# Reading layer 0's accumulators two pairs later, in a four-layer graph network on one core

## The chip, the core and the metric

One core of a Trainium2 chip runs the whole program in one launch. The metric is the device time of that launch in microseconds, taken over several executions; one execution is also recorded by the hardware profiler, and all rows below come from it. The engines are TensorE (PE, with its weight loads shown as PEld), VectorE (DVE), ScalarE (ACT), GpSimd (POOL) and SyncE (SP), which here only issues transfers.

## What is computed

`x` is 4096 x 128 and `adj` 4096 x 4096, both fp32. Four graph layers follow each other, each with a residual and a layer norm:

```python
x = _layernorm(x + _L0_gnn_ref(x, adj, L0_gnn_W), axis=-1)
x = _layernorm(x + _L1_gnn_ref(x, adj, L1_gnn_W, L1_gnn_b), axis=-1)
x = _layernorm(x + _L2_gnn_ref(L2_gnn_t, x, adj, L2_gnn_alpha, L2_gnn_beta), axis=-1)
x = _layernorm(x + _L3_gnn_ref(x, adj, L3_gnn_W_msg, ...), axis=-1)
```

Layer 0, which the change concerns, is a hyperbolic one. Its core is two products with the same matrix and then work on single rows:

```python
XW = mobius_matvec(W, X)
gamma = 2.0 / jnp.maximum(1.0 - jnp.sum(XW * XW, axis=-1, keepdims=True), EPS)
nominator = A_hat @ (gamma * XW)
denominator = _clamp_abs(A_hat @ (gamma - 1.0))
m = mobius_scalar_mul(0.5, nominator / denominator)
r = A_hat.sum(-1, keepdims=True)
return expmap0(jax.nn.relu(logmap0(mobius_scalar_mul(r, m))))
```

Layer 1 multiplies the same matrix, with degrees to the power -1/2 on both sides, by the new `x`.

## The kernel before

The adjacency matrix is cut into 8 slabs of 512 rows. TensorE needs it turned, so layer 0 turns each 128 x 128 block once, uses it, and stores it to `adj_t` in HBM; layers 1 and 3 load `adj_t` back.

**Layer 0's loop** is the same on all engines: `n` counts the pairs of column blocks, 16 pairs to a slab (`m = n % 16`), 128 in all. For each pair:
- SyncE loads tiles of 1 MB (L314), one for two pairs, a slab ahead, and stores the turned ones (L358) from three slots.
- TensorE turns eight blocks into one of two strips in PSUM (`turn0`, L473), four pairs ahead of the multiply (`AHEAD = 4`).
- ScalarE copies the strip into a slot of `full` (`full0`, L732), then writes its high part, rounded to fp32r, into `part_h` (`high0`, L739).
- VectorE writes the rest into `part_l` (`low0`, L1199).
- TensorE multiplies (`multiply0`, L490, L491 and L493), with `Y` (260 columns: 128 of data and two more, in high and low part) as the moving operand. The sums stand in four banks, the two of `acc` and the two of `mid`.

What ties the engines together: `turn0(n)` waits for `full0(n - 2)`, since there are two strips; `high0(n)` waits for `multiply0(n - 4)`, since `part_h` has eight slots; `multiply0(n)` waits for `low0(n)`; and the first multiply of a slab waits until the slab before has been read out.

**Reading the banks.** `read_acc0(s)` waits for the last multiply of slab `s`. ScalarE then copies two banks into `nat` (L745, L746) and VectorE the two others (L1206, L1207).

**The row chain.** From `nat` the slab's 512 rows go through some 40 small steps on ScalarE, VectorE and GpSimd (`rows0(k, s)`), each behind the one before by a semaphore that counts in the order of the list `ROWS`. The steps are hung into the next slab's loop by hooks: pair `m` runs `k = 2m` and `k = 2m + 1`. ScalarE has the square (L763), the logarithm (L767, with a table load), the relu (L771), a second square (L776) and the tanh (L780, with another table load). GpSimd has the sums (L974), the powers (L979, L981, L986, L989) and two products; VectorE everything else, from the degree steps (L1248 to L1253) to the layer norm. In the last slab GpSimd also scales `Y`'s groups for layer 1 (`y_scale`, L954) and writes their low parts (`y_low`, L961), and ScalarE writes their high parts (`y_high`, L723).

**Layer 1's loop** has 128 turns. ScalarE makes `high(1, n)` (L787), VectorE `low(1, n)` (L1320), TensorE multiplies (L512, L513, L521). The last slab's row chain is hung into its first 26 turns; ScalarE writes the last group of `Y` in turn 26.

Of the kernel before, what the change touches and what calls it, by code (L numbers as in the profile page):

```python
# [94 lines left out]
def build(nc, x, adj, w0, w1, b1, alpha, beta, w_msg, b_msg, w_ih, w_hh, b_ih, b_hh, out, scratch, dis_out):  # L95
    with ExitStack() as ctx:
# [584 lines left out]
        def _(act):  # L681
# [75 lines left out]
            def rows0(k, s):  # L757
                par = s % 2
                t, v, sc = t_of[par], v_of[par], sc_of[par]
                if k == 5:  # L760
                    act.wait_ge(row[par], row_before(0, s, "square"))
                    for q in range(Q):
                        last = act.activation(v[:, q, :], t[:, q, :], ACT.Square, accum_out=sc[:, SS, q:q + 1])  # L763
                    last.then_inc(row[par], 1)
                if k == 11:
                    act.wait_ge(row[par], row_before(0, s, "log"))
                    act.activation(sc[:, LOG, :], sc[:, RATIO, :], ACT.Ln).then_inc(row[par], 1)  # L767
                if k == 16:
                    act.wait_ge(row[par], row_before(0, s, "times_relu"))
                    for q in range(Q):  # L770
                        last = act.activation(t[:, q, :], t[:, q, :], ACT.Relu, scale=sc[:, SCL, q:q + 1])  # L771
                    last.then_inc(row[par], 1)
                if k == 17:
                    act.wait_ge(row[par], row_before(0, s, "square_u"))
                    for q in range(Q):
                        last = act.activation(v[:, q, :], t[:, q, :], ACT.Square, accum_out=sc[:, SS, q:q + 1])  # L776
                    last.then_inc(row[par], 1)
                if k == 19:
                    act.wait_ge(row[par], row_before(0, s, "tanh_u"))
                    act.activation(sc[:, H, :], sc[:, NRM, :], ACT.Tanh).then_inc(row[par], 1)  # L780
# [85 lines left out]
            for n in range(PAIRS * SLABS):  # L866
                s, m = n // PAIRS, n % PAIRS
                full0(n)
                high0(n)
                if s == 0 and 1 <= m <= GROUPS:  # L870
                    y_high(0, m - 1)
                if m == 1 and s > 0:
                    read_acc0(s - 1)
                if s > 0:
                    rows0(2 * m, s - 1)
                    rows0(2 * m + 1, s - 1)
                if s == SLABS - 1 and m >= 5 and m % 2 == 1:
                    y_high(1, (m - 5) // 2)
            read_acc0(SLABS - 1)
            for n in range(TURNS_ALL):  # L880
                high(1, n)
                if n == 4:
                    y_high(1, SLABS - 2)
                if 2 <= n < 26:
                    rows0(n + 1, SLABS - 1)
                if n == 26:
                    y_high(1, SLABS - 1)
                for k, s in hooks(1, n - ACT_LEAD):
                    rows1(k, s)
# [40 lines left out]
        def _(pool):  # L930
# [33 lines left out]
            def rows0(k, s):  # L964
                par = s % 2
                t, sc = t_of[par], sc_of[par]
                mine = slice(Q * s, Q * (s + 1))

                def before(name):
                    pool.wait_ge(row[par], row_before(0, s, name))  # L970
                if k == 3:
                    before("sum_parts")
                    pool.wait_ge(acc_read, acc_reads_done(0, s))
                    pool.tensor_tensor(t[:], nat[:, :, 0:D], nat[:, :, LO:LO + D], ALU.add).then_inc(row[par], 1)  # L974
                    before("sum_den")
                    pool.tensor_tensor(sc[:, DEN, :], nat[:, :, D], nat[:, :, LO + D], ALU.add).then_inc(row[par], 1)
                if k == 6:
                    before("norm")
                    pool.tensor_tensor(sc[:, NRM, :], sc[:, SS, :], half[:, 0:Q], ALU.pow).then_inc(row[par], 1)  # L979
                    before("deg_pow")  # L980
                    pool.tensor_tensor(sc[:, DEG, :], sc[:, SAFE, :], inv_half[:, 0:Q], ALU.pow).then_inc(row[par], 1)  # L981
                if k == 11:
                    before("dcol")
                    pool.tensor_tensor(dcol[:, mine], sc[:, DEG, :], sc[:, KEEP, :], ALU.mult).then_inc(row[par], 1)
                    before("dis")
                    pool.tensor_tensor(dis[:, mine], sc[:, ZERO, :], inv_half[:, 0:Q], ALU.pow).then_inc(row[par], 1)  # L986
                if k == 18:
                    before("norm_u")
                    pool.tensor_tensor(sc[:, NRM, :], sc[:, SS, :], half[:, 0:Q], ALU.pow).then_inc(row[par], 1)  # L989
                if k == 20:  # L990
                    before("times_u")
                    pool.tensor_tensor(t[:], t[:], wide(sc[:, SCL, :]), ALU.mult).then_inc(row[par], 1)
                    before("add_x")
                    pool.tensor_tensor(t[:], t[:], x_nat[:, mine, :], ALU.add).then_inc(row[par], 1)
                if k == 24:
                    layer_norm(0, s)
# [74 lines left out]
            for n in range(TURNS_ALL + HOOKS[1]):  # L1071
                if n < 24:
                    rows0(n + 3, SLABS - 1)
                if n == 4:
# [33 lines left out]
        def _(dve):  # L1108
# [127 lines left out]
            def rows0(k, s):  # L1236
# [8 lines left out]
                total = nat[:, :, D + 1]  # L1245
                if k == 5:
                    before("degrees")
# [5 lines left out]
                    dve.tensor_scalar(val(SIGN), val(DEN), 0.0, 2.0, ALU.is_ge, ALU.mult).then_inc(row[par], 1)  # L1253
                if k == 6:
                    before("abs_floor")
# [6 lines left out]
                                             ALU.mult).then_inc(row[par], 1)  # L1262
                if k == 8:
                    before("norm_den")
# [3 lines left out]
                    dve.tensor_scalar(val(UNIT_), val(NRM), MIN_NORM, None, ALU.max).then_inc(row[par], 1)  # L1268
                if k == 9:
                    before("artanh_a")  # L1270
# [7 lines left out]
                    dve.tensor_tensor(val(UNIT_), val(INV), val(INV_NRM), ALU.mult).then_inc(row[par], 1)  # L1278
                if k == 10:
                    before("ratio")  # L1280
# [4 lines left out]
                    dve.scalar_tensor_tensor(val(H), val(H), 1.0 / 3, val(Z), ALU.add, ALU.mult).then_inc(row[par], 1)  # L1285
                if k == 12:
                    before("series")
                    dve.scalar_tensor_tensor(val(SER), val(H), 1.0, val(CLIP), ALU.add, ALU.mult).then_inc(row[par], 1)
                if k == 13:
                    before("differ")  # L1290
# [3 lines left out]
                                             ALU.mult).then_inc(row[par], 1)  # L1294
                if k == 14:
                    before("artanh")
                    dve.scalar_tensor_tensor(val(ART), val(LOG), 0.5, val(SER), ALU.mult, ALU.add).then_inc(row[par], 1)
                    before("scale")
                    dve.scalar_tensor_tensor(val(SCL), val(ART), 0.5, total, ALU.mult, ALU.mult).then_inc(row[par], 1)
                if k == 15:  # L1300
                    before("scale_clip")
                    dve.tensor_scalar(val(SCL), val(SCL), ARTANH_MAX, -ARTANH_MAX, ALU.min, ALU.max).then_inc(row[par], 1)
                    before("scale_row")
                    dve.tensor_tensor(val(SCL), val(SCL), val(UNIT_), ALU.mult).then_inc(row[par], 1)
                if k == 18:
                    before("clamp_u")
                    dve.tensor_scalar(val(SS), val(SS), MIN_NORM ** 2, None, ALU.max).then_inc(row[par], 1)
                if k == 20:
                    before("inv_u")
                    dve.reciprocal(val(INV), val(NRM)).then_inc(row[par], 1)  # L1310
                    before("scale_u")
                    dve.tensor_tensor(val(SCL), val(H), val(INV), ALU.mult).then_inc(row[par], 1)
                if k in (22, 25):
                    layer_norm(0, (22, 25).index(k), s, lambda q: x_nat[:, Q * s + q, :])

# [138 lines left out]
            for n in range(PAIRS * SLABS):  # L1454
                s, m = n // PAIRS, n % PAIRS
                if s == 0 and m < GROUPS:
                    y_scale(m)
                low0(n)
                if m == 1 and s > 0:
                    read_acc0(s - 1)  # L1460
                if s > 0:
                    rows0(2 * m, s - 1)
                    rows0(2 * m + 1, s - 1)
            read_acc0(SLABS - 1)
            for n in range(TURNS_ALL):
                low(1, n)
                if n < 24:
                    rows0(n + 3, SLABS - 1)
                for k, s in hooks(1, n - DVE_LEAD):
                    rows1(k, s)  # L1470
# [59 lines left out]
```

## Time and profile before

| | |
|---|---|
| time, median of 3 runs | 1453.44 us (1452.11 to 1456.87) |
| profiled execution | 1456.6 us |
| its span in the trace | 1454.8 us |
| TensorE matmul busy | 1320.9 us (91%) |
| VectorE, ScalarE busy | 1072.7 us, 1073.5 us (74% each) |
| GpSimd busy | 570.1 us (39%) |
| mean granted TensorE clock | 0.969 of full |
| DMA, mean over the span | 284 GB/s |

The span is the time from the first to the last recorded instruction; the execution's own time holds some 1.8 us more. Layer 0's slabs lie between about 32 and 445 us. Matmuls are pipelined, so a busy TensorE is not one at its peak.

### The profile page before, as it was taken

Reading aid. Unit: us, or ns where it says so; the run is one execution under the profiler, and the core shown is the slowest. Engines: PE = TensorE matmul, PEld = TensorE weight load, DVE = VectorE, ACT = ScalarE, POOL = GpSimd, SP = SyncE. Lnnn points to the kernel's source line nnn. Section 1 sums busy time; section 2 is a strip of 40 time slices with the busy share of each in tenths; the row PEclk is TensorE's granted clock in tenths of the full one; section 3 lists DMA queues with packets and bytes.
Section 4 is the critical chain, followed back from the end, with each engine's and each line's share of the span. In section 5 each row is a group of like instructions: output and inputs, shape, how many; then the busy total and the mean of one; then the engine's idle time right before and its main releaser. Section 6 shows DMA issues by size and latency. Waiting matters only on the chain.

```text
span 1454.8 us, 21041 instructions
## 1 busy us (share of the span) xinstructions
PE 1320.9 (91%) x7640; PEld 1023.7 (70%) x7640; DVE 1072.7 (74%) x1936; ACT 1073.5 (74%) x1376; POOL 570.1 (39%) x441
## 2 busy tenths in 40 slices
PE   6998988998888989997799999999999889999995
PEld 5988988988887667774366666666666657767663
DVE  6844545555567889996687888978888869787874
ACT  6876877787687667774888888788887647767764
POOL 3312212221353544335177677676776650000010
PEclk9999999999999999999899999999999989999998
DMA  9998989989876878893578787787877848877850
GB/s 306 402 339 303 349 321 322 348 327 325 307 276 222 303 284 302 324 353 148 217 278 301 268 306 266 280 293 284 299 269 238 276 173 364 343 268 268 284 200 22
DMA packets 114808, 413.08 MB, mean 284 GB/s; under 512 B 10000, under 2 KB 23568, under 8 KB 90128
## 3 DMA queue, kind: packets, MB, share of 16 engines
q1 hardware_dynamic: 106256, 407.54, 77.3%
q10 hardware_dynamic: 8448, 4.20, 1.0%
q8 instruction: 60, 0.98, 0.3%
q14 instruction: 44, 0.36, 0.1%
HBM read 340.40 MB, written 71.30 MB: 283 GB/s over the span
## 4 chain that ended last, share of the span: by engine, by line
PE 53%; DVE 18%; ACT 17%; issue 6%; POOL 5%; DMA 1%; POOLq 0%; ACTq 0%; DVEq 0%; SPq 0%
DVE part_l L1320 7%; PE strip_b L576 5%; PE acc L493 5%; PE mid L493 5%; PE acc L521 4%; PE acc L512 4%; PE acc L513 4%; PE strip_b L473 3%; PE strip_a L473 3%; ACT part_h L787 3%; PE acc L593 3%; ACT arena L814 3%; PE acc L590 2%; PE acc L591 2%; ACT arena L732 2%
## 5 line engine op out<-in xcount | busy, mean ns | idle before, releaser
L1320 DVE TENSOR_TENSOR part_l<-arena,part_h 128x1024 fp32r<-128x1024 f32 x256 | 326.3, 1310 | 58.2 <-ACT part_h L787 56.9
L1033 POOL TENSOR_TENSOR part_l<-arena,part_h 128x512 fp32r<-128x512 f32 x237 | 303.8, 1294 | 156.1 <-ACT part_h L825 156.1
L787 ACT ACTIVATE part_h<-arena 128x1024 fp32r<-128x1024 f32 x256 | 264.7, 1055 | 120.9 <-PE acc L521 111.1
L1199 DVE TENSOR_TENSOR part_l<-arena,part_h 128x1024 fp32r<-128x1024 f32 x128 | 161.0, 1267 | 132.9 <-ACT part_h L739 132.1
L825 ACT ACTIVATE part_h<-arena 128x512 fp32r<-128x512 f32 x256 | 157.7, 623 | 94.4 <-DVE arena L1394 93.7
L512 PE MATMUL acc<-part_h,Y 128*128 128x512 f32 x512 | 220.6, 431 | 3.7 <-ACT part_h L787 3.3
L513 PE MATMUL acc<-part_h,Y 128*128 128x512 f32 x512 | 204.5, 399 | 0.0
L1001 POOL TENSOR_TENSOR sc<-sc,power 128x4 f32<-128x4 f32 x32 | 49.3, 1542 | 329.8 <-DVE sc L1225 329.8
L576 PEld LDWEIGHTS strip_b<-ident,arena 128*128 128x128 f32 x1024 | 127.0, 142 | 69.0 <-DVE arena L1394 19.5
L521 PE MATMUL acc<-part_l,Y 128*128 128x512 f32 x512 | 164.8, 403 | 11.1 <-DVE part_l L1320 10.8
L576 PE MATMUL strip_b<-ident,arena 128*128 128x128 f32 x1024 | 157.4, 277 | 15.7 <-DVE arena L1394 10.6
L739 ACT ACTIVATE part_h<-arena 128x1024 fp32r<-128x1024 f32 x128 | 135.6, 1060 | 31.3 <-PE mid L493 28.5
L493 PE MATMUL acc<-Y,part_h 128*128 128x260 f32 x496 | 145.3, 344 | 0.0
L493 PE MATMUL mid<-Y,part_h 128*128 128x260 f32 x496 | 144.1, 341 | 0.0
L814 ACT ACTIVATE arena<-arena,neg_peak 128x2048 f32<-128x2048 f32 x64 | 127.4, 1991 | 3.5 <-DVE neg_peak L1371 3.5
L820 ACT ACTIVATE arena<-arena,weight 128x2048 f32<-128x2048 f32 x64 | 127.1, 1991 | 2.4 <-DVE weight L1384 2.4
L491 PE MATMUL acc<-Y,part_l 128*128 128x130 f32 x512 | 127.5, 249 | 0.0
L521 PEld LDWEIGHTS acc<-part_l,Y 128*128 128x128 f32 x512 | 94.8, 190 | 40.5 <-DVE part_l L1320 20.1
L590 PE MATMUL acc<-part_h,Y 128*128 128x512 f32 x256 | 122.9, 480 | 0.0
L512 PEld LDWEIGHTS acc<-part_h,Y 128*128 128x128 f32 x512 | 98.0, 191 | 34.2 <-issue 7.2
L513 PEld LDWEIGHTS acc<-part_h,Y 128*128 128x128 f32 x512 | 98.0, 191 | 28.6 <-issue 8.4
L491 PE MATMUL mid<-Y,part_l 128*128 128x130 f32 x512 | 116.6, 228 | 0.0
(257 smaller groups left out, 2776.3 us busy)
## 6 DMA issues: line engine op xcount, KB each, us to landing
arena<-adj_t SPq DMA_DIRECT2D x128, 1024.0 KB, 4.9
arena<-in_adj SPq DMA_DIRECT2D x64, 1024.0 KB, 7.9
adj_t<-arena SPq DMA_DIRECT2D x64, 1024.0 KB, 6.3
arena<-in_adj SPq DMA_DIRECT2D x128, 512.0 KB, 5.9
part_h<-adj_t SPq DMA_DIRECT2D x64, 512.0 KB, 5.2
part_l<-adj_t SPq DMA_DIRECT2D x64, 512.0 KB, 5.6
scratch<-v ACTq DMA_DIRECT2D x8, 256.0 KB, 10.4
arena<-scratch SPq DMA_DIRECT2D x8, 256.0 KB, 5.3
```

The costliest lines, as they stand in the source:

```text
L491: last = pe.matmul(acc0[q][:, 0:LO], part_l[:, slot, mine], Y[:, j, 0:LO], start=False, stop=False)
L493: last = pe.matmul(acc0[q][:, 0:YW], part_h[:, slot, mine], Y[:, j, :], start=False, stop=stop)
L512: pe.matmul(to, Y[:, j, 0:D], h, start=j == 0, stop=False)
L513: pe.matmul(to, Y[:, j, LO:LO + D], h, start=False, stop=False)
L521: last = pe.matmul(to, Y[:, j, 0:D], part_l[:, 2 * (n % 4) + j % 2, :], start=False, stop=j == NB - 1)
L576: last = pe.transpose(strip_b[:, b % 2, P * q:P * (q + 1)], unit_in[:, place, P * (j % 8):P * (j % 8 + 1)], ident[:])
L787: act.activation(flat(part_h[:, slot:slot + 2, :]), turned_pair(n), ACT.Copy).then_inc(high_done, 1)
L814: act.activation(mine, mine, ACT.Exp, bias=neg_peak[:, r % 2:r % 2 + 1], accum_out=exp_sum[:, r % 2, h:h + 1]).then_inc(exps, 1)
L825: act.activation(part_h[:, b % 4, :], mixed[b % G_SLOTS], ACT.Copy).then_inc(high_done, 1)
L1033: pool.tensor_tensor(part_l[:, b % 4, :], mixed[b % G_SLOTS], part_h[:, b % 4, :].bitcast(F32), ALU.subtract).then_inc(low_done, 1)
L1199: dve.tensor_tensor(flat(part_l[:, slot:slot + 2, :]), full_pair(n), flat(part_h[:, slot:slot + 2, :]).bitcast(F32), ALU.subtract).then_in ...
L1320: dve.tensor_tensor(flat(part_l[:, slot:slot + 2, :]), turned_pair(n), flat(part_h[:, slot:slot + 2, :]).bitcast(F32), ALU.subtract).then_ ...
```

## The change

Three things move; no instruction is added or taken out.

1. The read of a slab's banks moves from pair 1 of the next slab, behind that pair's high and low part, to pair 3, on ScalarE between the copy and the high part, on VectorE ahead of the low part.
2. The hooks of the row chain move: the first GpSimd step from 3 to 7, the degree steps and the square from 5 to 8, the steps at 6 to 9, and every later one by two, which is one pair.
3. The last slab's read, so far ahead of all of layer 1, moves to turn 3 of layer 1, ahead of that turn's high and low part, and its hooks start one or three turns later.

```diff
@@ ScalarE, rows0 (square, log, relu, square_u, tanh_u)
-                if k == 5:
+                if k == 8:
...
-                if k == 11:
+                if k == 13:
...
-                if k == 16:
+                if k == 18:
...
-                if k == 17:
+                if k == 19:
...
-                if k == 19:
+                if k == 21:
@@ ScalarE, the loops
                 full0(n)
+                if m == 3 and s > 0:
+                    read_acc0(s - 1)
                 high0(n)
                 if s == 0 and 1 <= m <= GROUPS:
                     y_high(0, m - 1)
-                if m == 1 and s > 0:
-                    read_acc0(s - 1)
...
-            read_acc0(SLABS - 1)
             for n in range(TURNS_ALL):
+                if n == 3:
+                    read_acc0(SLABS - 1)
                 high(1, n)
...
-                if 2 <= n < 26:
-                    rows0(n + 1, SLABS - 1)
+                if 5 <= n < 26:
+                    rows0(n + 2, SLABS - 1)
@@ GpSimd, rows0 (sums; norm, deg_pow; dcol, dis; norm_u; times_u, add_x; layer norm)
-                if k == 3:
+                if k == 7:
...
-                if k == 6:
+                if k == 9:
...
-                if k == 11:
+                if k == 13:
...
-                if k == 18:
+                if k == 20:
...
-                if k == 20:
+                if k == 22:
...
-                if k == 24:
+                if k == 26:
@@ GpSimd, layer 1's loop
-                if n < 24:
-                    rows0(n + 3, SLABS - 1)
+                if 3 <= n < 24:
+                    rows0(n + 4, SLABS - 1)
@@ VectorE, rows0: 5 -> 8, 6 -> 9, 8 -> 10, 9 -> 11, 10 -> 12, 12 -> 14, 13 -> 15, 14 -> 16,
@@ 15 -> 17, 18 -> 20, 20 -> 22, (22, 25) -> (24, 27)
@@ VectorE, the loops
+                if m == 3 and s > 0:
+                    read_acc0(s - 1)
                 low0(n)
-                if m == 1 and s > 0:
-                    read_acc0(s - 1)
...
-            read_acc0(SLABS - 1)
             for n in range(TURNS_ALL):
+                if n == 3:
+                    read_acc0(SLABS - 1)
                 low(1, n)
-                if n < 24:
-                    rows0(n + 3, SLABS - 1)
+                if 3 <= n < 24:
+                    rows0(n + 4, SLABS - 1)
```

## Rows read from the trace of the kernel before

**Rows 1.** The page: busy time of each engine, share of the span, instructions

```profile
PE 1320.9 (91%) x7640; PEld 1023.7 (70%) x7640; DVE 1072.7 (74%) x1936; ACT 1073.5 (74%) x1376; POOL 570.1 (39%) x441
```

**Rows 2.** Timeline of ScalarE, first reads of slabs: start, length, instruction, [idle before <-releaser]

```profile
82.51 0.39 ACT L745 ACTIVATE arena<-acc 128x260 f32<-128x260 f32 x1 [4.33 <-PE mid L493]
...
135.06 0.39 ACT L745 ACTIVATE arena<-acc 128x260 f32<-128x260 f32 x1 [4.33 <-PE mid L493]
...
186.10 0.39 ACT L745 ACTIVATE arena<-acc 128x260 f32<-128x260 f32 x1 [4.33 <-PE mid L493]
...
390.26 0.39 ACT L745 ACTIVATE arena<-acc 128x260 f32<-128x260 f32 x1 [4.33 <-PE mid L493]
...
444.92 0.39 ACT L745 ACTIVATE arena<-acc 128x260 f32<-128x260 f32 x1 [5.78 <-PE mid L493]
```

**Rows 3.** Timeline of TensorE over one undisturbed pair: multiply, transposes, next multiply

```profile
127.47 0.31 PE L491 MATMUL acc<-Y,part_l 128*128 128x130 f32 x1
...
129.41 1.04 PE L473 MATMUL strip_a<-ident,arena 128*128 128x128 f32 x8
...
130.20 0.31 PE L491 MATMUL acc<-Y,part_l 128*128 128x130 f32 x1
```

**Rows 4.** Timeline of all engines at a slab's boundary

```profile
134.69 0.33 PE L493 MATMUL mid<-Y,part_h 128*128 128x260 f32 x1
...
135.41 0.42 DVE L1207 COPY arena<-mid 128x260 f32<-128x260 f32 x1
135.61 1.03 ACT L732 ACTIVATE arena<-strip_a 128x1024 f32<-128x1024 f32 x1
```

**Rows 5.** Timeline of TensorE: transposes that came behind a gap, in layer 0

```profile
111.48 1.94 PE L473 MATMUL strip_a<-ident,arena 128*128 128x128 f32 x8 [1.81 <-ACT arena L732]
136.79 1.06 PE L473 MATMUL strip_a<-ident,arena 128*128 128x128 f32 x8 [1.76 <-ACT arena L732]
141.63 1.62 PE L473 MATMUL strip_b<-ident,arena 128*128 128x128 f32 x8 [1.92 <-ACT arena L732]
164.02 1.06 PE L473 MATMUL strip_a<-ident,arena 128*128 128x128 f32 x8 [1.46 <-ACT arena L732]
...
398.10 1.97 PE L473 MATMUL strip_b<-ident,arena 128*128 128x128 f32 x8 [3.19 <-ACT arena L732]
```

**Rows 6.** Timeline of ScalarE in a middle slab: row steps and a high part

```profile
139.39 0.31 ACT L763 ACTIVATE v<-t 128x128 f32<-128x128 f32 x1 [1.66 <-DVE sc L1253]
...
155.70 1.28 ACT L771 ACTIVATE t<-t,sc 128x128 f32<-128x128 f32 x4
...
159.24 1.06 ACT L739 ACTIVATE part_h<-arena 128x1024 fp32r<-128x1024 f32 x1
...
162.75 0.21 ACT L780 ACTIVATE sc<-sc 128x4 f32<-128x4 f32 x1 [1.16 <-POOL sc L989]
```

**Rows 7.** Windows: busy us of each engine, granted TensorE clock, DMA share, GB/s

```profile
142.00:145.40 3.40, 3.40 (x19) 3.40 (x17) 2.42 (x6) 3.37 (x4) 0.84 (x1) 0.51 0.87 320
```

**Rows 8.** Windows, same columns (PE, PEld, DVE, ACT, POOL): a later slab and slab 0

```profile
136.80:186.10 49.30, 45.88 (x384) 45.31 (x384) 25.87 (x63) 37.30 (x56) 9.94 (x10) 0.97 0.92 329
32.00:82.50 50.50, 48.19 (x400) 46.95 (x400) 37.91 (x44) 40.34 (x44) 12.28 (x8) 0.97 1.03 396
```

**Rows 9.** Timeline of VectorE: from the powers to the ratio step

```profile
146.82 0.16 DVE L1265 TENSOR_TENSOR sc<-sc 128x4 f32<-128x4 f32 x1 [0.90 <-POOL sc L981]
...
147.94 1.22 DVE L1199 TENSOR_TENSOR part_l<-arena,part_h 128x1024 fp32r<-128x1024 f32 x1
...
149.33 0.16 DVE L1285 SCALAR_TENSOR_TENSOR sc<-sc 128x4 f32<-128x4 f32 x1
```

**Rows 10.** Timeline at layer 1's first multiply and at its copy of Y

```profile
446.58 0.50 PE L512 MATMUL acc<-part_h,Y 128*128 128x512 f32 x1 [1.70 <-ACT part_h L787]
...
491.69 0.63 ACT L723 ACTIVATE Y<-arena 128x512 fp32r<-128x512 f32 x1 [2.73 <-POOL arena L954]
```

## What I predict, before any run of the change

> **What bounds the kernel now.** I read the page first, then a table by stage, then layer 0 instruction by instruction. The page gives TensorE 91% of the span and VectorE and ScalarE 74% each [rows 1]: a busy kernel in which only stretches that one engine holds up can be won back. The change touches layer 0's slabs and the first turns of layer 1, so the question is what ends the waits there.
>
> ScalarE's reads of the accumulators mark the slabs [rows 2]. They stand 52.55 us apart for the first slab (82.51 to 135.06), 51.04 for the next (135.06 to 186.10), and the four after it repeat it (390.26 - 186.10 = 4 x 51.04). The last takes 54.66 (390.26 to 444.92). Undisturbed, TensorE needs 2.73 us for a pair: 1.94 from its first multiply to the next pair's transposes, and 0.79 from there to the next multiply (127.47, 129.41, 130.20) [rows 3]. Sixteen pairs make 43.7 us. So 51.04 - 43.7 = 7.3 us of each slab is not TensorE's own work at full clock.
>
> Where it goes is in the gaps. At the boundary TensorE's last matmul starts at 134.69, ScalarE and VectorE read the banks at 135.06 to 135.83, ScalarE's copy of the slab's third pair comes only then (135.61), and the transposes that need its strip start at 136.79, after 1.76 us idle [rows 2, 4, 5]. The next gap is 1.92 us before 141.63: ScalarE stood at a row step (square, L763) for VectorE until 139.39, and made the next copy 1.2 us later [rows 5, 6]. The third is 1.46 us before 164.02, behind the tanh step, which waited for GpSimd until 162.75 [rows 5, 6]. Together 5.1 us. The rest is mostly clock: after the 1.92 us gap the granted clock is 0.51, the lower level of 1.2 GHz, for 3.4 us [rows 7]. Half of that, 1.7 us, is work not done. What is left, 0.5 us, goes at the three restarts.
>
> Is something else just behind TensorE? Slab 0 shows what DMA carries: 396 GB/s over 50 us at full TensorE pace, where a later slab has 329 [rows 8]. A slab moves 16.8 MB (eight loads and eight stores of 1 MB), so DMA alone needs 16.8 / 396 = 42.4 us.
>
> **The change, part by part.** Times below count from the start of the accumulator read, T; "copy", "high" and "low" of pair i are L732, L739 and L1199, i counted from the slab's first pair.
>
> *The read moves from after high 1 to between copy 3 and high 3.* No instruction is added or removed: two reads on each of two engines, 0.55 us of ScalarE and 0.77 of VectorE. TensorE runs transposes four pairs ahead. Now transposes 4 need copy 2, which is queued behind the read. After the change copy 2 and copy 3 are done before the last multiply ends, so transposes 4 follow it without a gap, and the read lies beside them. Multiply 0 starts when the read is done, 0.88, where the transposes alone would allow 0.59. Today it starts at 2.52 (transposes at 136.79, plus 0.79). So the boundary costs 0.3 instead of 1.93. Were the cover of these transposes gone, the read would cost its whole 0.8. High 3 is behind the read on ScalarE, low 3 behind it on VectorE (1.65 to 2.87), but multiply 3 needs low 3 only at 9.1, so nobody waits.
>
> *The row steps go two hooks on, most of them one pair.* I walked them with today's durations. TensorE, unhindered, starts transposes i+5 at 2.84 + 2.73i, and copy i+3 must be out by then. High 4 waits for multiply 0 and runs 3.10 to 4.16; VectorE's low 4 ends at 5.43, and behind it come the degree steps until 5.79. ScalarE does the square at 5.82, copy 5 from 7.00 to 8.00. Transposes 7 are due at 8.30: the 1.92 us gap is gone, with 0.2 to spare. The wait itself (1.66 us on ScalarE) stays, only its place is covered.
> - Logarithm, now at pair 6. GpSimd's two powers end at 10.0 (today VectorE takes up behind them at 146.82), low 5 at 10.36, and VectorE's chain takes 1.12 us before the next low (146.82 to 147.94), so until 11.39; low 6 and the ratio step end 1.55 us later (147.94 to 149.33 plus 0.16) [rows 9], at 12.94; the logarithm goes at 12.98, copy 7 ends at 14.09, due 13.76: TensorE loses 0.48 with the restart. Today this step costs nothing in a middle slab, because TensorE is at half clock just then and ScalarE catches up.
> - Relu and second square, now at pair 9. Highs 7, 8 and 9 are end to end at 2.00 us a pair, the relu starts at 19.16, copy 10 ends 3.5 us later, as today (155.70, and the high behind it at 159.24 [rows 6]), at 22.67, due 22.43: 0.39 lost.
> - Tanh, now at pair 10: high 10 starts at 22.70, the tanh 3.51 us later as today (159.24 to 162.75 [rows 6]), and copy 11 ends at 27.33, due 25.55: 1.93 lost with the restart, against 1.46 today.
> - From there ScalarE at 2.00 us a pair regains its lead on 2.73 before the slab ends, as now. The layer norm's steps stay three pairs from the multiply that would need VectorE.
>
> The slab becomes 43.7 + 0.3 + 0.48 + 0.39 + 1.93 = 46.8 us for 51.04: **4.26 us** won. Five middle slabs give 21.3; the first, to the same 46.8, gives 5.8.
>
> *Last slab.* GpSimd also scales Y for layer 1 there (L954). Three of the six scalings now fall before the read, and the 3.19 us gap before 398.10 [rows 5] goes the same way as the 1.92 one. But VectorE's chain for the logarithm meets another scaling as it does today, and ScalarE has three Y copies of some 0.5 us among the steps. My walk has gaps of 0.25, 2.1, 1.5 and 1.9 us, 5.8 in all, where today's slab is 54.66 - 43.7 = 11.0 over the pure pace: 5.2 won, the least certain term.
>
> *Clock.* That sum of 32.3 us has today's clock losses taken out and none put in. In today's layer 0, gaps of 1.81, 1.92 and more were followed by the lower clock, and of those of 1.76 and below only one, the first boundary's ([rows 5] has gaps of either kind: the eight transposes behind them take 1.06 us at full clock, more at the lower). My tanh gap of 1.93 is on the edge, and the walk is good to some 0.3 us, so I let four of seven slabs pay 1.7: 6.7 us back. Bounds: none, or seven times 1.7 = 11.8.
>
> *Layer 1's entry.* High 0 to 2 and low 0 to 2 now run before T. The first multiply starts at 0.9 for 1.66 [rows 10]: 0.75 won. Against that, the row chain of slab 7 is about 0.6 us later in time while TensorE is a turn further, and ScalarE's copy of the last group of Y already waits 2.73 us for GpSimd at turn 26 [rows 10]; the multiply behind it starts when that copy is out. The gain can be given back there. Bounds -0.8 to +1.0, taken as 0. SP's loads for layer 1 wait for low 1, now some 5 us earlier; layer 1's pace is VectorE's, so this is worth nothing.
>
> Sum: 32.3 - 6.7 + 0 = 25.6 us. The profiled execution took 1456.6 us (span 1454.8 and 1.8 around it), so 1431.0. It lay 3.2 above the median of the three runs; against 1453.4 the forecast is **1428**.
>
> **A page's rule against it.** The Trainium skill (DMA: Bandwidth & Descriptors, Specifications) gives a limit of about 358 GB/s of HBM traffic for one core. By it a slab could not be shorter than 16.8 / 358 = 46.9 us, what the walk gives; the transfers would be at their limit all the time, the stores late, and rival 2 the likeliest case. The trace does not agree: slab 0 runs at 396 GB/s [rows 8].
>
> **Rivals.**
> 1. *No clock loss* (chance 0.17). The tanh gap stays under the edge: 1453.4 - 32.3 - 0.5 = 1421. For it: today's 1.46 to 1.76 gaps inside a running stretch kept the clock. Against: the walk says 1.93. The Trainium skill (TensorE: Matmul & The Clock Gate, Why this matters for your kernels) counts as harmful only idle gaps longer than any in these middle slabs. By it this rival would be the forecast, 1421. The trace does not agree: the clock fell behind a gap of 1.92 us [rows 5, 7].
> 2. *DMA or ScalarE takes the place of the boundary* (0.12). The stores wait in three slots, copy i waits for them, and at 360 GB/s for today's 329 they land later. If DMA settles between the two rates, at 340 to 346 GB/s, a slab is 48.5 to 49.4 us, which leaves 1.6 to 2.5 of the 4.26, over seven slabs 11 to 18 with the surplus of the first and last less what their clock costs: 1437 to 1443. Against it: slab 0.
> 3. *It does not do what it says* (0.04). If slabs were held by transfers at today's rate, 16.8 MB at 329 GB/s is 51 us and the time stays, 1453. The gaps end on ScalarE's copy, not on a load; that speaks against it.
> 4. *Slower* (0.04). ScalarE's queue fills. It is busy 37.3 us a slab [rows 8] and waits 3.4 at row steps; from 43.7 on it sets the pace instead of TensorE, and with 51.04 the change loses. That takes 10 us more of waiting for VectorE and GpSimd per slab; if norm and logarithm both fall a pair later than walked (2 x 2.7) and the tanh two pairs, a slab is 52 us and the time 1460.
>
> The forecast itself has 0.63. **Numbers.** Its own range: 32.3 - 11.8 - 1 = 19.5 won to 32.3 - 3.3 + 0.8 = 29.8, so 1424 to 1434. With rival 1's low end (1420) inside, and a margin toward rival 2 for the 0.3 us per step of the walk (7 x 0.6 = 4), 1419 to 1438. A difference under 0.3% (4.4 us) can hardly be told from none here; faster 0.92, same 0.04, slower 0.04.
>
> **What would show it.** Right: reads 46 to 49 us apart in layer 0; no gap over 0.4 us before the transposes that follow the read; ScalarE's wait at L763's line still about 1.7 us but no TensorE gap after it; a gap near 2 us behind the tanh; a lower clock after it in some slabs; layer 1's first multiply 0.9 after T. Wrong: copies that wait for a store; a gap behind the logarithm over 1 us in middle slabs; a boundary gap in place of the old one because high 2 or copy 3 is late. The prediction would be wrong above all if the three gaps of the walk, each the difference of two long sums, grew by 1 us each.

## The result, and the profile after

The changed kernel takes 1429.97 us (1428.33 to 1432.67, four runs) where the kernel before takes 1453.55 in the same comparison: the ratio is 0.9836, with a 95% interval of 0.9814 to 0.9859. The forecast was 1428, with 1419 to 1438 around it. The profiled execution has a span of 1428.0 us for 1454.8, so 26.8 less; the forecast was 25.6.

The timeline of ScalarE in the changed kernel, first read of each slab, as in [rows 2] (the line number is the same, 745):

```profile
82.40 0.39 ACT L745 ACTIVATE arena<-acc 128x260 f32<-128x260 f32 x1 [0.69 <-PE mid L493]
...
129.13 0.39 ACT L745 ACTIVATE arena<-acc 128x260 f32<-128x260 f32 x1 [0.69 <-PE mid L493]
...
175.87 0.39 ACT L745 ACTIVATE arena<-acc 128x260 f32<-128x260 f32 x1 [0.69 <-PE mid L493]
...
224.21 0.39 ACT L745 ACTIVATE arena<-acc 128x260 f32<-128x260 f32 x1 [0.69 <-PE mid L493]
...
367.64 0.39 ACT L745 ACTIVATE arena<-acc 128x260 f32<-128x260 f32 x1 [0.69 <-PE mid L493]
...
418.60 0.39 ACT L745 ACTIVATE arena<-acc 128x260 f32<-128x260 f32 x1 [2.27 <-PE mid L493]
```

The distances are 46.73 and 46.74 for the first two slabs, 48.34 for the third, and with the reads at 270.95 and 319.30, which are not shown, 46.74, 48.35 and 48.34 for the next three; the last takes 50.96. Two things are to be seen. Layer 0 gives 26.2 of the 26.8 us (336.2 between first and last read for 362.4) in this trace. And there are two kinds of middle slab, 1.6 us apart. ScalarE's idle time at the read fell from 4.33 to 0.69: it comes there with its other work done.

The timeline of all engines at a boundary, for [rows 4]: the transposes start right behind the last multiply, the reads (to 129.48 + 0.42) lie beside them, and the first multiply starts 0.91 us behind T = 129.13. TensorE idles 0.28 us for it, before its weight load (PEld).

```profile
128.76 0.34 PE L493 MATMUL mid<-Y,part_h 128*128 128x260 f32 x1
128.93 1.03 PE L473 MATMUL strip_a<-ident,arena 128*128 128x128 f32 x8
129.48 0.42 DVE L1208 COPY arena<-mid 128x260 f32<-128x260 f32 x1
...
130.01 0.19 PEld L490 LDWEIGHTS acc<-Y,part_h 128*128 128x128 f32 x1 [0.28 <-issue]
130.04 0.36 PE L490 MATMUL acc<-Y,part_h 128*128 128x260 f32 x1
```

All transposes of TensorE that came behind a gap between the reads at 129.13 and 175.87, for [rows 5], and one of the next slab:

```profile
143.29 1.09 PE L473 MATMUL strip_b<-ident,arena 128*128 128x128 f32 x8 [0.24 <-ACT arena L732]
151.95 1.06 PE L473 MATMUL strip_a<-ident,arena 128*128 128x128 f32 x8 [0.26 <-ACT arena L732]
156.52 1.09 PE L473 MATMUL strip_b<-ident,arena 128*128 128x128 f32 x8 [1.64 <-ACT arena L732]
...
203.25 1.93 PE L473 MATMUL strip_b<-ident,arena 128*128 128x128 f32 x8 [1.63 <-ACT arena L732]
```

The gaps of 1.76 and 1.92 us are gone. Three are left, behind logarithm, second square and tanh. The last row explains the slabs of 48.3: behind a gap of the same length the transposes took 1.93 us for 1.09. The windows behind the two gaps (columns as in [rows 7]) show the clock, 1.00 of full in the one and 0.50, the level of 1.2 GHz, in the other:

```profile
157.00:159.70 2.70, 2.70 (x26) 2.70 (x25) 1.58 (x4) 2.67 (x4) 0.52 (x1) 1.00 0.96 361
...
203.80:206.50 2.70, 2.70 (x15) 2.70 (x14) 1.66 (x4) 2.67 (x4) 0.59 (x1) 0.50 1.05 400
```

ScalarE's timeline of the slab, for [rows 6], to hold against the walk:

```profile
134.96 0.31 ACT L763 ACTIVATE v<-t 128x128 f32<-128x128 f32 x1 [1.66 <-DVE sc L1254]
...
142.12 0.21 ACT L767 ACTIVATE sc<-sc 128x4 f32<-128x4 f32 x1 [0.58 <-DVE sc L1286]
...
148.30 1.28 ACT L771 ACTIVATE t<-t,sc 128x128 f32<-128x128 f32 x4
...
155.35 0.20 ACT L780 ACTIVATE sc<-sc 128x4 f32<-128x4 f32 x1 [1.16 <-POOL sc L990]
155.46 1.00 ACT L732 ACTIVATE arena<-strip_b 128x1024 f32<-128x1024 f32 x1
```

Less T these are 5.83, 12.99, 19.17, 26.22 and 26.33. The walk had 5.82, 12.98, 19.16, 26.21 and 26.33.

The last slab is a case of its own. Its window, in the same columns, beside that of a middle slab:

```profile
129.13:175.87 46.74, 44.52 (x386) 43.74 (x385) 26.88 (x64) 38.88 (x58) 11.50 (x10) 1.00 0.96 359
...
367.64:418.60 50.96, 44.35 (x352) 43.13 (x350) 32.69 (x65) 38.16 (x61) 28.29 (x20) 0.93 0.69 268
```

TensorE has 352 matmuls there for the 386 of a middle slab: the transposes run four pairs ahead, so the last four pairs of the layer have none beside them. And the clock is 0.93 of full, with two low stretches, 0.55 over 3.6 us behind a gap of 2.85 us (384.40) and 0.70 over 5.6 us behind one of 1.96 us (413.01). That is some 3.3 us of work not done.

### The profile page after: what moved, and what is told of

It is laid out like the page before. It is cut to its first block, busy times and chain, and to the rows that moved or that the text cites. A ratio compares the mean times of both kernels' runs of the same rounds, so it can differ in the third digit from the quotient of the medians.

```text
span 1428.0 us, 21041 instructions
## 1 busy us (share of the span) xinstructions
PE 1315.2 (92%) x7640; PEld 1017.7 (71%) x7640; DVE 1076.5 (75%) x1936; ACT 1072.9 (75%) x1376; POOL 577.5 (40%) x441
## 4 chain that ended last, share of the span: by engine, by line
PE 50%; DVE 19%; ACT 18%; issue 7%; POOL 4%; DMA 2%; POOLq 0%; ACTq 0%; DVEq 0%; SPq 0%
DVE part_l L1321 7%; PE strip_b L576 5%; PE acc L521 4%; PE acc L512 4%; PE acc L513 4%; PE acc L493 3%; PE mid L493 3%; ACT arena L732 3%; PE acc L593 3%; ACT arena L814 3%; DVE part_l L1200 3%; ACT part_h L787 2%; PE acc L590 2%; PE acc L591 2%; PE strip_b L473 2%
```

## The experiments

Each kernel was timed against the kernel before on the same chip. Nothing in them leaves out any of the computation.

**1. The read alone undone.**

```diff
                 full0(n)
-                if m == 3 and s > 0:
-                    read_acc0(s - 1)
                 high0(n)
...
+                if m == 1 and s > 0:
+                    read_acc0(s - 1)
```

The same on VectorE, behind `low0(n)`.

> The changed kernel with the read of layer 0's banks put back behind the high part of the second pair, on both engines, and nothing else undone: the row hooks stay two on, layer 1's entry stays as changed. Theory (the boundary gap is the copy of the third pair queued behind the read): the 1.76 us gap before the transposes behind each read comes back, reads of neighbouring slabs lie 1.5 to 2 us further apart than in the changed kernel (48.3 to 50.5 us for 46.7 to 48.3), the 1.9 us gap behind the square stays away, and the time is 1430 + 7 x 1.7 = 1442. Rival (the gain is the hooks' and not the read's): time within 3 us of 1430. Rival (the two belong together, since the later square needs the later read): the square's gap comes back too, reads 51 us apart, 1450.

It took 1444.57 us, ratio 0.9926 (0.9905 to 0.9947). TensorE's transposes behind gaps, in the slab whose read is at 182.09:

```profile
183.81 1.06 PE L473 MATMUL strip_a<-ident,arena 128*128 128x128 f32 x8 [1.76 <-ACT arena L732]
192.67 1.09 PE L473 MATMUL strip_b<-ident,arena 128*128 128x128 f32 x8 [0.50 <-ACT arena L732]
```

The boundary gap is back to the hundredth, at every slab. The gap behind the square is 0.50 at most and not 1.92: the hooks alone keep most of it away, and the later read takes the rest. Slabs are 49.2 to 50.9 us apart. So both rivals fall. The read is worth 1444.57 - 1430, some 15 us, a little over the 12 expected, since the 0.50 came with it and five of the six slabs before the last lost clock here (granted 0.97 in each), and three in the changed kernel.

**2. The read behind the high part, on ScalarE only.**

```diff
-                if m == 3 and s > 0:
-                    read_acc0(s - 1)
                 high0(n)
...
+                if m == 3 and s > 0:
+                    read_acc0(s - 1)
```

> The changed kernel with ScalarE's read behind the fourth pair's high part instead of ahead of it; VectorE's read and all hooks as changed. Theory (the first multiply of a slab waits for the read alone, and the transposes cover 0.8 us of it): ScalarE's high part takes 1.0 us first, so the multiply starts at about 1.85 us behind the end of the last multiply instead of 0.9; 1 us per slab, less what ScalarE's later gaps give back (the first, 0.24, would go): 7 x 0.7 to 1 = 5 to 7 us, 1435 to 1437. Rival (the order inside the pair is free, what counts is that two copies are out): within 2 us of 1430.

It took 1431.55 us, ratio 0.9836 (0.9818 to 0.9854), the changed kernel's own. By the time the rival wins. The trace says otherwise. The timeline at a boundary:

```profile
133.80 0.36 PE L490 MATMUL acc<-Y,part_h 128*128 128x260 f32 x1 [0.98 <-ACT arena L746]
```

TensorE stands 0.98 us for ScalarE's read at each of the seven boundaries, and the slabs are 47.62 us apart where the changed kernel's undisturbed ones are 46.74: the order costs 0.9 us a slab, as the theory had it. It doesn't show in the time because this kernel lost clock in one slab before the last (49.25 us), and the changed kernel in three, and because its last slab is 49.32 for 50.96: from the first read to the last the two differ by 0.5 us. All four of its runs have a mean granted clock of 0.977 or 0.978, the changed kernel's have 0.967 to 0.974, so this is not the profiled run alone. The 0.24 us behind the logarithm did not go (0.25), and the tanh gap is 1.64 or 1.65 us as in the changed kernel. A window behind the one at 160.26, where the clock stayed at 1.00:

```profile
160.00:163.50 3.50, 3.24 (x29) 3.24 (x30) 1.64 (x4) 3.44 (x5) 0.58 (x1) 1.00 0.81 300
```

**3. The read one pair earlier.** `m == 2` for `m == 3`, on both engines.

> The changed kernel with the read at the third pair instead of the fourth, between copy and high part, on both engines; hooks as changed. Theory (ScalarE stands in its queue at the read until the last multiply ends, and has 2 us less done when it does): the transposes behind the read have their copy, so no boundary gap; but copy 5, behind the square, comes at 9.5 us for 8.3 due: a gap of 1 to 1.3 us there, of which the later gaps give back part; reads 0.3 to 1.3 us further apart than in the changed kernel, 1432 to 1439. Rival (any pair from the third on does the same): within 2 us of 1430.

1433.75 us, ratio 0.9856 (0.9836 to 0.9877); the interval overlaps that of the changed kernel, so the difference in time is not settled by it. In the trace slabs are 48.2 us apart at full clock (four of six), 1.45 more than 46.74, and the gap behind the square is there:

```profile
140.49 1.09 PE L473 MATMUL strip_b<-ident,arena 128*128 128x128 f32 x8 [1.08 <-ACT arena L732]
```

Walked: 1.0 to 1.3. But the later gaps gave nothing back, against the theory, and the logarithm's is 0.42 for 0.24; so the slabs lie 1.45 us further apart where 0.3 to 1.3 was expected. The other two of the six lost clock (49.8 us, granted 0.97), one fewer than in the changed kernel. The rival is refuted by the trace, not by the time.

**4. The tanh one pair later still.** In slabs 0 to 6:

```diff
-                if k == 21:
+                if k == (23 if s < SLABS - 1 else 21):
                     act.wait_ge(row[par], row_before(0, s, "tanh_u"))
```

Behind it on VectorE 22 becomes 24 and (24, 27) becomes (26, 29), on GpSimd 22 becomes 24 and 26 becomes 28.

> The changed kernel with the tanh and every row step behind it one more pair later, in slabs 0 to 6 only. Theory (the gap of 1.64 us behind the tanh is ScalarE waiting 1.16 us for GpSimd's power while it is 2.5 us behind from relu and square): the wait is gone, ScalarE has a pair more to catch up, the gap is under 0.3 us; reads 44.6 to 45.0 us apart in slabs 0 to 5, none at the lower clock: 6 slabs x 1.9 plus three clock losses of 1.6, and something of the last: 1430 - 14 to 17 = 1413 to 1416. Rival (ScalarE's work as such is the bound, so the gap only moves): reads 46.5 to 48.4 us apart as now, within 3 us of 1430. Rival (DMA takes over, 16.8 MB in 44.8 us being 375 GB/s): reads near 46 us apart with copies waiting for stores, 1425.

1413.95 us (1409.98 to 1418.17), ratio 0.9718 (0.9689 to 0.9747). No single run lies near that median: two took 1410 to 1411 us at a mean granted clock of 0.979, two 1417 to 1418 at 0.968 and 0.969, so the hit in the expected 1413 to 1416 is partly chance. The profile is of the 1410.85 us run. ScalarE's timeline at the tanh:

```profile
152.10 1.28 ACT L780 ACT_TABLE_LOAD   x1
153.39 0.20 ACT L780 ACTIVATE sc<-sc 128x4 f32<-128x4 f32 x1
153.50 1.01 ACT L732 ACTIVATE arena<-strip_a 128x1024 f32<-128x1024 f32 x1
```

It stands behind its table load alone and no longer waits for GpSimd; no TensorE gap follows. The six slabs are 44.94 to 44.96 us apart, 1.8 less, and none is at the lower clock (1.00 from 81.37 to 351.05). This settles the transfers too. One slab of it:

```profile
127.00:171.00 44.00, 43.42 (x378) 42.89 (x377) 26.20 (x63) 38.21 (x56) 11.52 (x10) 1.00 1.00 370
```

370 GB/s, and the gaps left (0.25 and 0.26) end on ScalarE's copies behind row steps. It beats both kernels.

**5. On top of it, GpSimd scales Y ahead of the read.**

```diff
-                if s == SLABS - 1 and m < SLABS - 2:
-                    y_scale(m)
+                if s == SLABS - 1 and m < 3:
+                    y_scale(2 * m)
+                    y_scale(2 * m + 1)
```

> The kernel with the late tanh, and in the last slab GpSimd scales Y's six groups in the first three pairs, two to a pair, so ahead of the read, instead of one to a pair in the first six. Theory (the 2.85 us gap behind the last slab's logarithm is VectorE's chain slowed by two scalings beside it, 3.7 us for 1.1): the gap falls to 0.3 to 0.6, the last slab from 48.8 to 46.3 us or less, 2.5 us (4 with a clock loss saved): 1410 to 1412. Rival (the Y copies on ScalarE make that gap): it stays over 2 us, time 1414 as before.

1411.85 us, ratio 0.9706 (0.9691 to 0.9722), which can't be told from experiment 4. It lies in the expected 1410 to 1412, but not by the theory. That holds for the gap behind the last slab's logarithm, 0.73 us for 2.85, which also refutes the rival, and not for the sum: the last slab takes 50.13 us where 46.3 or less was expected, and from the read that ends slab 5 (307.09, for 306.11) to the last (403.37, for 399.86) it takes 96.3 us, in experiment 4 93.8. VectorE's timeline says why:

```profile
345.88 4.02 DVE L1234 TENSOR_SCALAR arena<-t,sc 128x128 f32<-128x128 f32 x4
349.82 5.46 DVE L1201 TENSOR_TENSOR part_l<-arena,part_h 128x1024 fp32r<-128x1024 f32 x4
355.21 0.42 DVE L1208 COPY arena<-mid 128x260 f32<-128x260 f32 x1
```

The end of the former slab's layer norm, 1.12 us elsewhere, takes 4.02 beside five scalings; the lows pile up and VectorE reads its banks 2 us after ScalarE (353.24). The conflict was moved, not removed.

**6. And the square a hook earlier.** `k == 7` for 8 in slabs 0 to 6, on ScalarE and for the degree steps on VectorE, on top of 5.

> As the kernel before it, and in slabs 0 to 6 the degree steps and the square are one hook earlier, at the fourth pair, right behind the read. Theory (the two gaps of 0.24 behind the logarithm and the second square are what ScalarE is late by): low 3 ends at 2.87, the square runs from 3.3 to 4.5, copy 4 ends at 5.5 with 5.57 due, everything behind is up to a pair ahead; both gaps go, reads are 44.0 to 44.2 us apart for 44.95: 6 x 0.9 = 5 us, 1405 to 1407. Rival (the square's 1.7 us wait now hits the copy that has least to spare): a new gap of 0.3 to 1 us at copy 4, reads 44.5 to 45.5 apart, no gain.

1417.20 us, ratio 0.9741 (0.9722 to 0.9761): slower than 5, so the rival wins, and more than it says. Slabs are 45.8 apart for 44.95. TensorE's gaps in one of them:

```profile
134.12 1.06 PE L473 MATMUL strip_a<-ident,arena 128*128 128x128 f32 x8 [0.29 <-ACT arena L732]
143.11 1.09 PE L473 MATMUL strip_b<-ident,arena 128*128 128x128 f32 x8 [0.62 <-ACT arena L732]
```

The square's wait is now 2.06 us and falls where one copy less is out. The logarithm comes later and not earlier, 13.83 us behind T for 12.99: high 4 now stands behind the square, VectorE's low 4 waits for it until 135.09 (6.98 behind T, for 4.20 in experiment 4), the steps ahead of GpSimd's powers stand behind low 4, and the powers start at 8.85 for 7.87.

```profile
135.09 1.22 DVE L1201 TENSOR_TENSOR part_l<-arena,part_h 128x1024 fp32r<-128x1024 f32 x1 [3.35 <-ACT part_h L739]
```

I had walked copy 4 to 5.5 us with 5.57 due; it came at 5.9 (132.97 + 1.00, T being 128.11).

**7. Layer 1's entry undone**, the read ahead of layer 1's loop and the last slab's hooks a turn earlier.

> The changed kernel with the last slab's read back ahead of layer 1's loop on both engines, and the last slab's hooks a turn earlier to fit; layer 0's slabs as changed. Theory (layer 1's entry won 0.75 us at the first multiply, and half of it was given back behind): 0 to 1.5 us slower than the changed kernel, the first multiply 1.66 us behind the read for 0.9. Rival (the entry is worth nothing, its gap only moves): no difference.

1430.66 us, ratio 0.9833 (0.9815 to 0.9850): it can't be told from the changed kernel (1429.97). That fits the rival, and the theory's 0 to 1.5 us as well; the intervals reach 2.5 to 3 us either way. Its first multiply has the gap of 1.70 us of [rows 10] again, where the profiled run of the changed kernel has 0.95:

```profile
419.15 0.50 PE L512 MATMUL acc<-part_h,Y 128*128 128x512 f32 x1 [1.70 <-ACT part_h L787]
```

```profile
419.51 0.47 PE L512 MATMUL acc<-part_h,Y 128*128 128x512 f32 x1 [0.95 <-DVE arena L1208]
```

The first of these rows is of the experiment, the second of the changed kernel. The 0.75 us are there in that one execution only. In the second execution of the changed kernel (experiment 8) TensorE idles longer at this point than in the kernel before, and its first multiply stands 2.04 us behind T for 1.66:

```profile
416.94 0.47 PE L512 MATMUL acc<-part_h,Y 128*128 128x512 f32 x1 [2.08 <-DVE arena L1208]
```

There VectorE was still at a low part of layer 1 (from 414.21, 1.92 us) when the last multiply ended, and read its banks only at 416.05, 1.15 us behind T (414.90). In experiments 1 and 3 the first multiply is 2.0 us behind T too. With the read ahead of layer 1's loop no low part of layer 1 can stand before it.

**8. The changed kernel once more.**

> The changed kernel unchanged, another execution, to see whether the same slabs lose the clock. Theory (a gap of 1.64 us costs the clock or not by how it lies in time against the clock's own rhythm, not by its length): slabs are 46.7 or 48.3 us, none in between, but not all in the same order as before. Rival (it hangs on the slab, its data or its transfers): 48.3 us again in the third, fifth and sixth.

1430.67 us, ratio 0.9830 (0.9808 to 0.9853). In this execution's trace the slabs are 46.75, 46.76, 48.34, 46.75, 48.40 and 46.75: as in the first trace for five of them, but the sixth, 48.34 there, is at full clock here. The gap before it is 1.65 us in both. The last slab is 48.71 for 50.96. So the same code, slab and gap can lose the clock or not; the slabs alone don't decide it. Nor is it random: experiment 7, whose slabs 0 to 6 are hooked alike, loses it in the third, fifth and sixth again, so 17 of the 18 slabs of the three traces agree. What repeats was not found.

From the first read to the last this execution takes 332.5 us for 336.2, but from there to the end 1016.0 for 1009.4, in layers that are the same code. Parts of single traces thus differ by several us without any change to the kernel.

**9. The later steps back**, read, sums, degree steps, square and powers as changed. The logarithm and every step behind it stand at their old hooks; the artanh and ratio steps ahead of it at 10 and 11, one hook earlier than changed and one later than before.

> The changed kernel, read and first steps (sums, degrees, square, powers) as changed, but every step from the artanh on back at its old hook, one pair earlier. Theory (the chain needs the pair: VectorE's ratio step is done at 11.8 us however it is hung): ScalarE stands at the logarithm at pair 5 until then, copy 6 ends at 12.9 with 11.0 due, a gap of 1.6 to 1.9 us before transposes 8 that the changed kernel doesn't have; relu, square and tanh lose about as much as there; slabs 48.0 to 48.6 us at full clock for 46.74, 7 x 1.6 = 11 and some clock losses more: 1440 to 1446. Rival (the later hooks of the rest are worth nothing, read and square bring it all): within 3 us of 1430. Rival (a shorter chain is better): 1425.

1439.19 us, ratio 0.9895 (0.9878 to 0.9912), just under the expected band. Slabs of 48.5 to 49.2, and the gap the theory wanted, a little longer than the 1.6 to 1.9 us expected:

```profile
146.08 1.06 PE L473 MATMUL strip_a<-ident,arena 128*128 128x128 f32 x8 [2.05 <-ACT arena L732]
```

The later hooks of the rest are thus worth some 9 us of the 23.6, beside the 15 of the read. The slab with this gap, and with one of 1.82 us behind the tanh, kept the full clock:

```profile
132.85:181.39 48.54, 44.52 (x386) 43.77 (x385) 27.04 (x64) 38.90 (x58) 11.50 (x10) 1.00 0.96 347
```

## Why the prediction was right, and where it was off

**The boundary.** Right: the first multiply 0.91 us behind T for a forecast of 0.88, and the gap before the transposes gone. Experiment 1 brings it back alone. TensorE idles 0.28 us for a forecast of 0.3; in experiment 2, where the high part takes the time beside the transposes, it idles 0.98.

**The row chain.** Right to 0.01 us at all five steps of ScalarE that the walk names. The traces of experiments 3 and 9 show that both halves of the fit are needed, the late read with ScalarE's work done and the late steps.

**The middle slabs.** 46.8 forecast, 46.74 measured at full clock; the first slab 5.82 won for 5.8.

**The clock: near the size, by luck, from a wrong rule.** I let four of seven slabs pay 1.7 us for the tanh gap, 6.7 in all. Three of the six slabs before the last paid, 1.6 each; the last paid some 3.3, but behind two other gaps and not behind the tanh's. That is 8.1. And I got to my number by the length of the gap, with an edge between 1.76 and 1.81 us, which does not hold. First, I set 1.93 us, with the restart in it, against rows that give the idle time without it; like for like the walk's gap is the measured 1.64, below my edge, and by my own rule no slab would have paid. Second, gaps of 1.63 to 1.65 us were followed by full clock and by half, in one kernel (156.52 and 203.25) and in one slab of two executions (experiment 8). Third, gaps of 2.05 and 1.82 us, above the edge, kept the full clock in experiment 9. What decides remains open; these only say that the length of the gap is not enough. Rival 1 failed by the clock, not by its gap. It is the largest thing that could have gone wrong unseen: with none or all seven of the tanh gaps paying, the changed kernel would by my estimate (1.6 us each) have taken 1425 or 1436.

The Trainium skill (TensorE: Matmul & The Clock Gate, Why this matters for your kernels) counts only longer idle gaps as harmful. The trace of the changed kernel does not agree either: the clock fell behind gaps of 1.63 to 1.65 us in three of six slabs, and in experiment 4, where these gaps are gone, in none of the six.

**The last slab.** The mis-sized term. 5.2 us were forecast with the clock taken out, which makes a slab of 49.5. Measured are 50.96 with 3.3 of clock loss in it, so 47.7, and 7.0 won; in experiment 8 it is 48.71 with 3.4 (two low stretches again), so 45.3, and 9.4 won. The step that was wrong is the pure pace. I took 43.7 us, sixteen pairs with transposes, where four pairs have none and take 1.86 for 2.73 (407.19 to 409.05), 3.5 less in all. The gaps went the other way: 6.5 us idle, without the restarts, for 5.8 with them. The one behind the square went, as said. The logarithm's is 2.85 for my 2.1 (the chain beside GpSimd took 3.7 us where it took 2.8 before), the tanh's 1.65, and there is one that the walk didn't have, before a multiply near the end:

```profile
413.01 0.33 PE L491 MATMUL acc<-Y,part_l 128*128 128x130 f32 x1 [1.96 <-DVE part_l L1200]
```

VectorE's layer norm of the former slab came a pair later, its last step took 2.05 us (from 409.78) beside low parts of Y on GpSimd, where it takes 1.12 alone, and low 14 was late (411.74). I had said of that norm that it stays three pairs from the multiply that needs VectorE; in the last slab that is false. In experiment 8 the step took 1.12 and this gap is not there, but the clock fell behind the tanh's gap, which it did not in the first trace. Where it fell there (experiments 1, 3 and 8) the gap near the end is missing, where it held (changed kernel, 2 and 7) it is there with 1.95 or 1.96.

So the sum of 25.6 came out close to 26.2 with two misses in it that nearly cancel in the first trace: 34.3 us were won for 32.3 before the clock, and 8.1 lost to it for 6.7.

**Layer 1's entry.** Taken as 0; experiment 7 finds no difference within its interval of 2.5 us either way. But the 0.75 us named for the first multiply is not a property of the change: 0.91 behind T in one execution, 2.04 in the other, for 1.66 before. I had let high 0 to 2 and low 0 to 2 run before T; in the second execution VectorE had not finished low 2 by then.

**The rivals.** Rivals 2 and 3: in the changed kernel ScalarE never stands idle ahead of a copy (L732, all 128 of them), so none waited for a store, and the undisturbed slabs move 359 GB/s and more; at 370 GB/s over 44 us (experiment 4) no gap of TensorE ends on a transfer. The limit of 358 GB/s in the Trainium skill (DMA: Bandwidth & Descriptors, Specifications) is passed there too; the measurement decides. Rival 4: ScalarE's waits at the square and the tanh were 1.66 and 1.16, as before the change, and at the logarithm 0.58; no slab before the last took more than 48.4.

**What is left over.** 26.2 us in layer 0 leaves 0.5 of the 26.8 behind it, which two single traces can't assign: the changed kernel's own two differ there by 6.6 us (experiment 8).

## What to carry to other kernels

A read that must wait for the end of a phase belongs as late in its engine's queue as the next phase's first need allows, behind whatever the other engines need first; here a copy of 1 us behind it cost 1.76 us of TensorE each time. When an engine's queue repeats, walk it with measured durations against the due times of the engine it feeds: this held to 0.01 us in the slab walked through above, and it also named the next gap, whose removal (a step hooked one pair later) was worth another 16 us. But hold like against like when a sum is compared with a row, and walk the odd last round by itself, with the work that it really has, since that is where the sum failed. And look at a second trace of the same kernel before explaining a difference of a few us in one part of it.

## What was not expected of the hardware

The length of a gap does not say whether TensorE's lower clock follows. Gaps of 1.63 to 1.65 us cost nothing in some slabs and 1.6 us in others, through half rate for some 3 us, and three traces agree on 17 of 18 slabs as to which; gaps of 2.05 and 1.82 us cost no clock in one slab (experiment 9). Two kernels whose undisturbed slabs differ by 0.9 us (experiment 2 and the changed one) so come out at the same time. Where gaps of this size remain, a difference of 5 us between kernels says little without the granted clock of each slab.

Elementwise work on GpSimd and VectorE at the same time can stretch either. VectorE's four layer-norm outputs took 1.12 us in a middle slab and 4.02 beside five scalings (experiment 5), each of which kept its 1 us. In the changed kernel one scaling on GpSimd took 1.03 us alone (370.74) and 5.36 beside VectorE's low parts (411.90), which kept their 1.2.
